# The split-adjacency stage turned round: weights first, fp32r halves, one bank a batch

## What is computed

```python
adj_0 = jnp.diag(jnp.diagonal(adj))
adj_1 = jnp.triu(adj, k=1)
adj_2 = jnp.tril(adj, k=-1)
h = jnp.einsum('bjf,kfo->kbjo', x, W)            # W: (3, 128, 128)
out = (jnp.einsum('ij,bjo->bio', adj_0, h[0]) + jnp.einsum('ij,bjo->bio', adj_1, h[1])
       + jnp.einsum('ij,bjo->bio', adj_2, h[2]))
return out + bias[None, None, :]
```

## Time and profile before

| | before |
|---|---|
| median of 3 runs | 1361.2 us (1360.2 to 1361.8) |
| profiled execution | 1360.81 us, span 1359.1 us |
| mean granted TensorE clock | 0.976 |
| TensorE busy | 1223.1 us, 90% (weight loads 1062.9 us) |
| VectorE busy | 1010.1 us, 74% |
| ScalarE busy | 768.4 us, 57% |
| GpSimd busy | 491.5 us, 36% |

### The profile page before, as it was taken

How to read it: one execution, slowest core, us unless ns; L and a number is a source line. 1 busy time by engine, 2 the same in 40 slices (tenths; PEclk the granted TensorE clock), 3 DMA queues, 4 the chain that set the end, 5 groups by cost and what they waited for, 6 DMA issues and landing times. The chain is left out here.

```text
span 1359.1 us, 25823 instructions
## 1 busy us (share of the span) xinstructions
PE 1223.1 (90%) x8194; PEld 1062.9 (78%) x8194; DVE 1010.1 (74%) x2860; ACT 768.4 (57%) x1660; POOL 491.5 (36%) x675
## 2 busy tenths in 40 slices
PE   2899999999999998999997999979999788867998
PEld 1778787787887878878776777869999777756998
DVE  6677877768677687786775899977777488876766
ACT  3575675766757757577575777752222166652332
POOL 3121311313213131131221222237888478841332
PEclk8899999999999999999999999989999899998999
DMA  9200000000000000000000000000000000001222
GB/s 273 76 1 1 1 1 0 0 0 0 0 0 0 0 0 0 0 0 0 1 1 1 1 0 0 0 1 1 0 0 0 1 2 1 2 1 31 69 72 75
DMA packets 24710, 20.87 MB, mean 15 GB/s; under 512 B 1745, under 2 KB 20305, under 8 KB 24401
## 3 DMA queue, kind: packets, MB, share of 16 engines
q1 hardware_dynamic: 24656, 20.21, 5.2%
HBM read 11.82 MB, written 8.39 MB: 15 GB/s over the span
## 5 line engine op out<-in xcount | busy, mean ns | idle before, releaser
L581 ACT ACTIVATE gate<-ps,b_lstm 128x256 f32<-128x256 f32 (+2 forms) x624 | 300.3, 558 | 42.1 <-PE ps L608 42.1
L606 PE MATMUL ps<-H_hi,w_hi 128*128 128x256 f32 (+2 forms) x624 | 212.6, 342 | 29.9 <-ACT gate L581 18.2
L479 POOL TENSOR_TENSOR hid_lo<-hid,hid_hi 128x256 fp32r<-128x256 f32 (+2 forms) x96 | 87.9, 915 | 345.6 <-DVE hid L547 345.6
L607 PE MATMUL ps<-H_hi,w_lo 128*128 128x256 f32 (+2 forms) x624 | 205.3, 330 | 0.0
L608 PE MATMUL ps<-H_lo,w_hi 128*128 128x256 f32 (+2 forms) x624 | 195.1, 334 | 6.8 <-DVE H_lo L550 6.5
L606 PEld LDWEIGHTS ps<-H_hi,w_hi 128*128 128x128 f32 x624 | 117.6, 188 | 55.8 <-ACT gate L581 25.5
L591 ACT ACTIVATE tanh_c<-cell 128x512 f32<-128x512 f32 (+2 forms) x176 | 90.4, 514 | 124.3 <-DVE cell L540 83.0
L608 PEld LDWEIGHTS ps<-H_lo,w_hi 128*128 128x128 f32 x624 | 115.3, 189 | 22.5 <-DVE H_lo L550 10.3
L607 PEld LDWEIGHTS ps<-H_hi,w_lo 128*128 128x128 f32 x624 | 117.9, 189 | 7.8
L606 PE MATMUL ps<-hid_hi,w_hi 128*128 128x256 f32 (+2 forms) x384 | 119.2, 317 | 0.8 <-DVE hid_hi L546 0.8
L607 PE MATMUL ps<-hid_hi,w_lo 128*128 128x256 f32 (+2 forms) x384 | 117.3, 312 | 0.0
(11 more groups left out here) (203 smaller groups left out, 3213.5 us busy)
## 6 DMA issues: line engine op xcount, KB each, us to landing
out<-x SPq DMA_DIRECT2D x32, 256.0 KB, 2.3
w_raw<-in_WihT SPq DMA_DIRECT2D x1, 1024.0 KB, 8.3
w_raw<-in_WhhT SPq DMA_DIRECT2D x1, 1024.0 KB, 8.5
wqkvT<-in_WqkvT SPq DMA_DIRECT2D x1, 192.0 KB, 5.2
w_sb<-in_W SPq DMA_DIRECT2D x1, 192.0 KB, 5.0
ends_row<-in_src_row SPq DMA_DIRECT2D x1, 128.0 KB, 3.5
ends_row<-in_dst_row SPq DMA_DIRECT2D x1, 128.0 KB, 4.3
x<-in_x_in SPq DMA_DIRECT2D x8, 0.5 KB, 10.4
```

The source lines that it names most:

```text
L479: nc.gpsimd.tensor_tensor(h_lo, h32, h_hi.bitcast(F32), ALU.subtract).then_inc(sa(g, "a_lo"), 1)
L581: nc.scalar.activation(gate[:, g, z, 0:w * GB], gate_bank(g, k, m)[:, 0:w * GB], ACT.Tanh if z == G else ACT.Sigmoid, bias=b_lstm[:, 4 * ( ...
L606: nc.tensor.matmul(dst, w_hi[:, src, p - 1, z], v_hi, start=start, stop=False)
L607: return nc.tensor.matmul(dst, w_lo[:, src, p - 1, z], v_hi, start=False, stop=False)
```

## The change

Layer three is turned round: for each batch the input is multiplied with all three weight matrices first, laid side by side as one operand of 384 columns (`w2_hi`, `w2_lo`), and the adjacency parts come after, for four batches at once.

- TensorE per round: four transposes (`HT2`); for each batch three accumulated fp32r products of 384 columns with the halves of the transposed input as the stationary operand (`MIX`), each batch in a bank of its own (banks 2 to 5, one set); two accumulated fp32 products of 512 columns with the two adjacency parts (`OUT2`, banks 6 and 7 in turn).
- ScalarE writes the high half of the transposed input with the ReLU in it, VectorE the low half. Columns 128 to 383 of the four banks (the terms of U and L) go to `hw` by ScalarE in two instructions of two banks; columns 0 to 127 (the diagonal's) are multiplied with `diag_col` and added to `xb` by VectorE, also in two, starting with the other two banks; each waits for the other's first before it takes the second half (`OWN` and `MIX`).
- The normalisation of the next turn, with its ReLU, moves from VectorE and GpSimd to ScalarE (`APPLY2`); GpSimd also makes the shift, -mean x rstd (`SCALE2`).
- The order is `IN_TURN`, with `MIX` and `OWN` one round behind, `OUT2` two.
- In the preparation the weights of layer three are split too, and the diagonal becomes a column by a reduction; the product L358 goes. `pipeline` takes the list as an argument, and layer two passes `BESIDE`.

The functions that are replaced stand above; this is the new side.

```diff
@@ preparation, VectorE
+                dve.wait_ge(S["w_high"], 4)
+                link(nc.vector.tensor_tensor(w2_lo[:], w2_sb[:].rearrange("p k o -> p (k o)"), w2_hi[:].bitcast(F32),
+                                             ALU.subtract))
...
-                link(nc.vector.tensor_copy(diag_bc[:], ps[:, 2, 0:P]))
+                link(nc.vector.tensor_reduce(diag_col[:], adj_diag[:], AXX, ALU.add))
@@ preparation, ScalarE and TensorE
+                nc.scalar.activation(w2_hi[:], w2_sb[:].rearrange("p k o -> p (k o)"), ACT.Copy).then_inc(S["w_high"], 1)
...
-                nc.tensor.matmul(ps[:, 2, 0:P], ones[:], adj_diag[:], start=True, stop=True)
@@ layer three
+        IN_TURN = [(HT2, 0), (XB, 0), (MIX, 1), (OWN, 1), (OUT2, 2), (STATS2, 0), (SCALE2, 0), (APPLY2, 1)]
+
+        def bank2(what, g):
+            return ps[:, {HT2: 0, OUT2: 6}[what] + g % 2]
@@ GpSimd
+                    if what == XB:
+                        if before:
+                            pool.wait_ge(S["c_o"], count - W1 + 1)
+                        nc.gpsimd.tensor_tensor(xb[:, g * QB:(g + 1) * QB], x[:, bass.ds(i * NB + g * QB, QB), :],
+                                                bias2_bc[:].unsqueeze(1).to_broadcast([P, QB, C]),
+                                                ALU.add).then_inc(S["c_xb"], 1)
+                    elif what == SCALE2 and more:
...
+                        wait_apart(pool, S["c_aggr"], count * QB + QB)
+                        if before:
+                            wait_apart(pool, S["c_hn"], (count - W1 + 1) * QB)
+                        nc.gpsimd.tensor_scalar(r, mv[:, of, 1], EPS, None, ALU.add).then_inc(S["c_var"], 1)
+                        nc.gpsimd.tensor_scalar(sh, mv[:, of, 0], -1.0, None, ALU.mult).then_inc(S["c_nmean"], 1)
+                        pool.wait_ge(S["c_var"], count + 1)
+                        nc.gpsimd.tensor_tensor(r, r, half[:, 0:QB], ALU.pow).then_inc(S["c_rstd"], 1)
+                        pool.wait_ge(S["c_nmean"], count + 1)
+                        pool.wait_ge(S["c_rstd"], count + 1)
+                        nc.gpsimd.tensor_tensor(sh, sh, r, ALU.mult).then_inc(S["c_shift"], 1)
@@ VectorE
+                    if what == HT2:
+                        dve.wait_ge(S["c_hTh"], count + 1)
+                        nc.vector.scalar_tensor_tensor(hT2_lo[:, g % 2], by4(bank2(HT2, g)), 0.0,
+                                                       hT2_hi[:, g % 2].bitcast(F32),
+                                                       ALU.max, ALU.subtract).then_inc(S["c_hTl"], 1)
+                    elif what == OWN:
+                        dve.wait_ge(S["c_xb"], count + 1)
+                        dve.wait_ge(S["c_wp"], count + 1)
+                        for k in (1, 0):
+                            if k == 0:
+                                dve.wait_ge(S["c_hw"], 2 * count + 1)
+                            own = xb[:, g * QB + 2 * k:g * QB + 2 * k + 2]
+                            nc.vector.scalar_tensor_tensor(own, ps[:, 2 + 2 * k:4 + 2 * k, 0:C], diag_col[:], own,
+                                                           ALU.mult, ALU.add).then_inc(S["c_own"], 1)
+                    elif what == OUT2:
+                        dve.wait_ge(S["c_own"], 2 * count + 2)
+                        dve.wait_ge(S["c_op"], count + 1)
+                        nc.vector.tensor_tensor(x[:, bass.ds(i * NB + g * QB, QB), :], by4(bank2(OUT2, g)),
+                                                xb[:, g * QB:(g + 1) * QB], ALU.add).then_inc(S["c_o"], 1)
+                    elif what == STATS2 and more:
+                        norm_stats((i + 1) * NB + g * QB, 0, QB, S["c_stats"], g * QB)
+                        wait_apart(dve, S["c_stats"], count * QB + QB)
+                        if before:
+                            wait_apart(dve, S["c_shift"], count - W1 + 1)
                         norm_aggr(g * QB, QB, S["c_aggr"])
@@ ScalarE
+                    if what == HT2:
+                        act.wait_ge(S["c_hTp"], count + 1)
+                        nc.scalar.activation(hT2_hi[:, g % 2], by4(bank2(HT2, g)), ACT.Relu).then_inc(S["c_hTh"], 1)
+                    elif what == MIX:
+                        act.wait_ge(S["c_wp"], count + 1)
+                        if before or g > 1:
+                            act.wait_ge(S["c_op"], count - 1)
+                        for k in range(2):
+                            if k == 1:
+                                act.wait_ge(S["c_own"], 2 * count + 1)
+                            nc.scalar.activation(hw[:, g % 2, :, 2 * k:2 * k + 2].rearrange("p k b o -> p b k o"),
+                                                 ps[:, 2 + 2 * k:4 + 2 * k, C:3 * C].rearrange(
+                                                     "p b (k o) -> p b k o", k=2), ACT.Copy).then_inc(S["c_hw"], 1)
+                    elif what == APPLY2 and more:
+                        act.wait_ge(S["c_hTp"], count + 1)
+                        act.wait_ge(S["c_shift"], count + 1)
+                        for j in range(g * QB, (g + 1) * QB):
+                            nc.scalar.activation(hn[:, j],
+                                                 x[:, bass.ds((i + 1) * NB + j, 1), :].rearrange("p a c -> p (a c)"),
+                                                 ACT.Relu, bias=shift[:, j:j + 1],
+                                                 scale=rstd[:, j:j + 1]).then_inc(S["c_hn"], 1)
@@ TensorE
+                    if what == HT2:
+                        if before:
+                            pe.wait_ge(S["c_hn"], (count - W1 + 1) * QB)
+                        if before or g > 1:
+                            pe.wait_ge(S["c_hTl"], count - 1)
+                        for b in range(QB):
+                            ins = nc.tensor.transpose(bank2(HT2, g)[:, b * T:(b + 1) * T], hn[:, g * QB + b], ident[:])
+                        ins.then_inc(S["c_hTp"], 1)
+                    elif what == MIX:
+                        pe.wait_ge(S["c_hTl"], count + 1)
+                        if before or g > 0:
+                            pe.wait_ge(S["c_hw"], 2 * count)
+                            pe.wait_ge(S["c_own"], 2 * count)
+                        for b in range(QB):
+                            dst = ps[:, 2 + b, 0:3 * C]
+                            nc.tensor.matmul(dst, hT2_hi[:, g % 2, b], w2_hi[:], start=True, stop=False)
+                            nc.tensor.matmul(dst, hT2_hi[:, g % 2, b], w2_lo[:], start=False, stop=False)
+                            ins = nc.tensor.matmul(dst, hT2_lo[:, g % 2, b], w2_hi[:], start=False, stop=True)
+                        ins.then_inc(S["c_wp"], 1)
+                    elif what == OUT2:
+                        pe.wait_ge(S["c_hw"], 2 * count + 2)
+                        if before or g > 1:
+                            pe.wait_ge(S["c_o"], count - 1)
+                        for k in range(2):
+                            ins = nc.tensor.matmul(bank2(OUT2, g), adj_ul[:, k],
+                                                   hw[:, g % 2, k].rearrange("p b o -> p (b o)"),
+                                                   start=(k == 0), stop=(k == 1))
+                        ins.then_inc(S["c_op"], 1)
```

More of the change, by code:

```diff
@@ L716, in four_layers, with pipeline @@
         BESIDE = [(HT, 0), (PT, 2), (QK, 0), (VAL, 0), (EXP, 1), (SCORE, 0), (STATS, 0), (OUT1, 2), (APPLY, 1)]
-        def pipeline(engine, stage):
+        def pipeline(engine, stage, beside):
             def turn(i, first, last):
                 for step in range(W1):
-                    for what, behind in BESIDE:
+                    for what, behind in beside:
                         g = step - behind
@@ L732, in pipeline @@
             turn(TURNS - 1, False, True)
-            for step in range(max(behind for _, behind in BESIDE)):
-                for what, behind in BESIDE:
+            for step in range(max(behind for _, behind in beside)):
+                for what, behind in beside:
                     if behind > step:
@@ L897, in _ @@
             def _(pool):
[L898 to L920, removed]
+                def stage(i, what, g, more, before):
+                    count = i * W1 + g
+                    if what == XB:
[5 more added lines that the diff above has]
+                    elif what == SCALE2 and more:
+                        of = slice(g * QB, (g + 1) * QB)
+                        r, sh = rstd[:, of], shift[:, of]
+                        wait_apart(pool, S["c_aggr"], count * QB + QB)
[8 more added lines that the diff above has]
+                        nc.gpsimd.tensor_tensor(sh, sh, r, ALU.mult).then_inc(S["c_shift"], 1)
@@ L922, in _ @@
+                pipeline(pool, stage, IN_TURN)
             @block.vector
             def _(dve):
[L924 to L939, removed]
@@ L944, in aggr, with stage @@
                         norm_aggr(g * QB, QB, S["c_aggr"])
[L946 to L950, removed]
```

(13 more changed lines are left out.)

38 lines of the change are left out of this document (14 added, 24 removed).

## The result

| | before | after |
|---|---|---|
| median | 1361.5 us (4 runs) | 1343.38 us (1342.24 to 1343.9, 4 runs) |
| ratio | | 0.9863, 95% interval 0.9852 to 0.9875 |
| profiled execution | 1360.81 us, span 1359.1 | 1343.16 us, span 1341.3 |
| granted clock | 0.976 | 0.983 |
| TensorE, VectorE, ScalarE, GpSimd busy | 1223, 1010, 768, 491 us | 1207, 1008, 836, 457 us |

The account below looks back on a forecast made before the run. TensorE's issue time was taken as the bound: 0.44 + 2.10 + 1.72, say 4.27 us a round against 4.84. With start and end, 17.15 us off 1360.8 gives 1343.7, plus 0.4 for the median: 1344, range 1341 to 1349.

Parts of the forecast that it names:

- The bound and the sum per round: Layer three: TensorE's issue time bounds each of 32 rounds, falling from 4.84 to 4.27 us.
- The forecast: Whole kernel: 17.15 us gained in layer three, median 1344 us; range 1341 to 1349, chance 0.62.
- About 0.4 us of slack: Layer three's rounds: TensorE stays the bound with about 0.4 us to spare, so waits were costed at nothing.
- The exchange: ScalarE and VectorE emptying banks 2 to 5: 1.58 us, hidden behind 2.16 us of other TensorE work.
- 0.15 us of wait, which its slack takes: ScalarE's wait for GpSimd's shift, ready some 4.1 us after the adjacency products and asked for at 3.95.
- VectorE's share: VectorE's operations in a layer three round: 3.61 us, below TensorE's 4.27.
- The start: Layer three's first rounds: transposes at 911.65, first products 914.2 at half clock, clock back about 921, first adjacency products ended 924.2.
- The preparation: Splitting layer three's weights: no cost; 0.55 us if it isn't hidden, 1 with a GpSimd collision.
- Rival 1: Layer three's exchange doesn't fit, ScalarE's copies 0.30 to 0.34 us longer: 6 to 9 us lost, 1350 to 1353; chance 0.17.
- Rival 2: GpSimd's passes block VectorE in layer three, 7.0 us a round: 67 us lost, 1428; chance 0.04.
- Rival 3: TensorE pauses each layer three round, clock falls to 1.2 GHz, round 8.5 us: 115 us lost, 1476; chance 0.02.
- Rival 4: More gain in layer three: 4.18 us a round, clock back at 919, 4 us more, 1340 or 1339; chance 0.10.

Follow-up runs that it names:

- E1: Kernel after with one of layer three's three mixed products (high half of the input times low half of the weights) left out: 1333.28 us.
- E4: Kernel after with the mixed products in fp32, one product of 384 columns a batch in place of three fp32r ones: 1358.01 us.
- E7: Kernel after with ScalarE's normalisation of layer three two rounds behind in place of one, VectorE's order untouched: 1341.36 us.
- E8: Kernel after with the normalisation two rounds behind and the product of high half and low weights left out: 1325.96 us in one run.
- E5: Kernel after with the normalisation of layer three back on VectorE, the ReLU staying where the transposed input is read: 1351.4 us.
- E6: Kernel after without the exchange of halves, VectorE taking its diagonal terms after both of ScalarE's copies: 1351.81 us.

## Why the prediction was right, point by point

- **The bound and the sum per round.** Right for TensorE's sum; the loop through the shift comes out 0.05 us above it (E1). Products of 384 columns every 0.173 us (0.175 taken), fp32 with 512 columns 0.43, the sum 4.24 (4.27 taken). E4's 4.74 shows that rounds follow such sums also in fp32.
- **The forecast** of 1344 against 1343.4, gain 17.15 against 17.8 us. Mean round 4.281, 0.01 above the one used: two errors that cancel, 0.03 too much for TensorE's sum and 0.04 too little for waits costed at nothing. That the forecast is so close is in part luck.
- **"About 0.4 us of slack".** Wrong, the step that failed. In the kernel after there was next to none: E1 takes 0.69 us from TensorE's sum and gets 0.23. The exchange by itself was sized well: once the shift is early, 0.35 us is spare in most rounds of E7, whose order on VectorE is the predicted one, and without a TensorE that binds the round is 3.77 (E8). What ate the slack is the path of the shift. I had "0.15 us of wait, which its slack takes"; I checked the exchange and each engine's sum, but did not follow this path until it closes on itself, nor put the hand-offs into it. Its terms were mis-sized: the shift was to be ready 4.1 us after the adjacency products; from their end at 983.17 to ScalarE's start at 988.24 it is 5.07. The rows of after show where the rest is:

```profile
983.59 0.69 DVE L939 TENSOR_TENSOR x<-ps,xb 128x512 f32 x1 [0.39 <-PE ps L1006]
...
985.40 0.38 DVE L108 BATCH_NORM_AGGREGATE mv<-stats 128x2 f32<-128x6 f32 x4 [0.35 <-DVE stats L102]
...
986.14 0.23 POOL L908 TENSOR_SCALAR rstd<-mv 128x4 f32<-128x4 f32 x1 [1.00 <-DVE mv L108]
```

  0.42 until the addition starts; 0.35 before the ends of the statistics, where 0.15 was taken; 0.36 from VectorE to GpSimd (985.78 to 986.14); 0.21 from GpSimd to ScalarE (988.03 to 988.24). VectorE's row came out longer too: its first diagonal term starts 3.41 us after the adjacency products' end (983.17 to 986.58), and 3.09 in most rounds of E7, where 2.9 was taken. The consequence was small only because the loop came out 0.05 us above TensorE's sum and not more.
- **VectorE's share.** 3.61 us a round and near the limit: right; E5 adds the normalisation and it becomes the bound. A diagonal term lasts 0.476, not 0.42.
- **The start.** Nearly right. Transposes at 911.51 (911.65), first products at 914.01 (914.2) at half the clock, every 0.32, the second ones at 919.36 (919.7) after the one open exchange. The granted clock is 0.50 from 917.0 to 917.5 and 1.00 from 917.7 on, not from 921; that is most of the 0.9 us by which the first adjacency products ended earlier (923.26, 924.2).
- **The preparation.** Nothing, as said: the added subtraction, with its two SBUF inputs, took 0.56 us and was not held up; GpSimd's select L248 beside it took 0.53 us where it took 0.29 before. The next block started 0.70 us after the queue of SP had finished:

```profile
26.39 10.31 SPq L208 DMA_DIRECT2D x<-in_x_in  x3
...
32.79 0.56 DVE L317 TENSOR_TENSOR w_lo<-w_sb,w_hi 128x384 fp32r<-128x384 f32 x1
...
36.12 0.20 ACT L348 ACTIVATE log_a<-rank 128x2 f32<-128x2 f32 x1 [6.57 <-DVE rank L332]
37.40 1.83 PE L663 MATMUL ps<-adjT_sb,hn 128*128 128x128 f32 x7 [2.69 <-PEq L189]
```

- **Rival 1** (the exchange doesn't fit) was the nearest miss: it does not fit in about half of the rounds, by up to 0.18 us, through the shift and not through slow copies, whose median is 0.597 us.
- **Rival 2** (GpSimd blocks VectorE): no. The 32 last additions took 691 to 693 ns, the 64 diagonal terms 474 to 484.
- **Rival 3** (the clock): no. After has 1.00 in the middle of the stage (925 to 1035), and so has E6, with a pause of some 0.3 us in every round of 4.56. The Trainium skill, TensorE: Matmul & The Clock Gate, on psum-queue depth-cycling, says that short idles between groups of matmuls that cycle through banks can make the clock swing; in these two traces it did not.
- **Rival 4** asked for 4.18 a round and the clock back at 919; the clock came, the round didn't.

## What to carry to other kernels

Sums per engine and the longest single wait are not enough: where two engines hand work to each other more than once in a round, follow the chain until it closes on itself, over as many rounds as it takes, and add every hand-off. Where an engine waits for several others, compare its start with the end of each of them: the one that a view names need not be the one. Shortening the bound engine's work is also the test for it: take out a part, and see how much of it comes back. A short chain on a slow engine that everybody waits for (here three operations on four numbers) should be put a whole round ahead; it costs one digit in a list. Here that is worth only 1.3 us, but it decides what a further saving on TensorE brings: with one product less it is worth 7.8 (the layer in E8 against E1, one trace each).

## What the runs showed of the hardware

- An fp32r product with 384 columns starts every 0.173 us and an fp32 instruction with 384 every 0.32; as fp32 takes two of these, three fp32r products (0.52) are cheaper than one fp32 product (0.64). That is where 15 of the 18 us come from.
- From VectorE's last result to GpSimd's start it takes 0.08 to 0.09 us with a plain wait (layer four of after, 1068.34 to 1068.43), 0.20 with one wait that also raises a counter (`wait_apart`; three rounds of layer three's first turn) and 0.29 to 0.37 with two of them (its other turns, 985.78 to 986.14 among them). Which part of `wait_apart` costs this was not tried.
- A copy out of two PSUM banks in pieces of 256 elements takes 577 to 599 ns (after, L964), as one of 512 elements out of a single bank does (571 to 601, L956).
